# Three chunks of a projection in three fp32r matmuls, with the high part kept in the convolution's buffer

## What is computed

```python
conv = conv_b + sum(x_pad[:, k:k + L, :] * conv_w[k, 0] for k in range(K))   # K = L = 128
proj = conv @ Wp + bp                       # 512 -> 2 * 64
B_t, C_t = softplus(proj[..., :N]), tanh(proj[..., N:])
u = x @ Ws + bs
state = decay * state + dt * b_t * u_t;  y_t = c_t * state      # scan over time
x = x + y @ Wo + bo
h_next = tanh(h @ Wh + (x @ Wx + b)[t])                         # scan over time
out = x + h_next
```

## Time and profile before

| | |
|---|---|
| Runs | 1198.05 us median of 3 (1197.93 to 1198.36) |
| Profiled execution | 1197.2 us, of which the span of the trace is 1195.0 us |
| Granted PE clock, mean | 0.995 of full |
| Convolution of a chunk, 1st / others | 32.0 us / 29 to 30 us |
| Projection of a chunk, first transpose to the end of its last matmul | 41.6 us (chunk 2: 41.55) |
| First transpose of the four projections, at | 44.81, 116.53, 188.19, 259.74 us |
| Recurrence stage, from | 300.9 us |

### The profile page before, as it was taken

One profiled execution on the slowest core, in us unless ns is written; L12 is line 12 of the kernel. 1 busy time (PEld: TensorE's weight loads), 2 busy tenths in 40 slices (PEclk: granted clock), 3 DMA queues, 4 the chain that ended last, 5 costly groups with the idle time before them and its releaser, 6 DMA issues.

```text
span 1195.0 us, 16884 instructions
## 1 busy us (share of the span) xinstructions
PE 1164.7 (97%) x5888; PEld 938.6 (79%) x5888; DVE 682.7 (57%) x1104; ACT 532.8 (45%) x768; POOL 326.7 (27%) x175
## 2 busy tenths in 40 slices
PE   5999999999799999999999999999999999999997
PEld 5769587785588888888888888888888888888886
DVE  5565565556755555655555655555555555655553
ACT  2443535446235454544545354545445453545431
POOL 1000000014333333444333333334443333333340
PEclk9999999999899999999999999999999999999999
DMA  9909266261222222222322222222223222222202
GB/s 317 331 5 349 72 207 219 71 233 36 71 71 71 71 71 70 70 70 71 100 89 91 70 70 70 70 70 70 70 79 96 91 85 70 70 70 71 71 36 70
DMA packets 81462, 121.17 MB, mean 101 GB/s; under 512 B 3936, under 2 KB 39776, under 8 KB 81440
## 3 DMA queue, kind: packets, MB, share of 16 engines
q1 hardware_dynamic: 81440, 120.87, 31.1%
HBM read 87.30 MB, written 33.55 MB: 101 GB/s over the span
## 4 chain that ended last, share of the span: by engine, by line
PE 96%; DVE 1%; POOL 1%; DMA 1%; ACT 0%; issue 0%; SPq 0%; POOLq 0%; DVEq 0%
PE bank L639 10%; PE bank L708 10%; PE bank L716 10%; PE bank L717 10%; PE bank L720 10%; PE bank L702 10%; PE bank L701 9%; PE bank L660 9%; PE bank L652 5%; PE bank L744 5%; PE bank L691 2%; PE bank L683 2%; PE bank L692 2%; PE bank L677 2%; POOL x_lo L311 1%; DMA vec<-vectors 1%
## 5 line engine op out<-in xcount | busy, mean ns | idle before, releaser
L311 POOL TENSOR_TENSOR x_lo<-x_f,x_hi 128x512 fp32r<-128x512 f32 x126 | 159.5, 1297 | 561.9 <-ACT x_hi L403 561.9
L416 ACT ACTIVATE h_f<-z_f 128x512 f32<-128x512 f32 x128 | 80.9, 632 | 294.7 <-DVE z_f L588 294.7
L716 PE MATMUL bank<-wh_hi,hT_hi 128*128 128x512 f32 x512 | 200.4, 391 | 0.0
L702 PE MATMUL bank<-wx_lo,x_hi 128*128 128x512 f32 x512 | 200.2, 391 | 0.0
L717 PE MATMUL bank<-wh_lo,hT_hi 128*128 128x512 f32 x512 | 200.2, 391 | 0.0
L701 PE MATMUL bank<-wx_hi,x_hi 128*128 128x512 f32 x512 | 199.6, 390 | 0.0
L598 DVE TENSOR_TENSOR hT_lo<-bank,hT_hi 128x512 fp32r<-128x512 f32 x128 | 88.6, 692 | 187.0 <-ACT hT_hi L420 187.0
L588 DVE TENSOR_TENSOR z_f<-bank,b_rows 128x512 f32<-128x512 f32 x128 | 88.5, 692 | 130.3 <-PE bank L720 129.0
L305 POOL TENSOR_TENSOR x_lo<-x_f,x_hi 128x2048 fp32r<-128x2048 f32 x32 | 148.3, 4634 | 11.9 <-PE bank L652 11.9
L708 PE MATMUL bank<-wx_hi,x_lo 128*128 128x512 f32 x512 | 144.5, 404 | 1.5 <-DVE x_lo L581 1.1
L720 PE MATMUL bank<-wh_hi,hT_lo 128*128 128x512 f32 x512 | 137.0, 389 | 0.0
(11 more groups left out here) (71 smaller groups left out, 1472.2 us busy)
## 6 DMA issues: line engine op xcount, KB each, us to landing
x_ring<-x_rev SPq DMA_DIRECT2D x64, 512.0 KB, 8.0
x_f<-x_dtb SPq DMA_DIRECT2D x32, 1024.0 KB, 8.3
out<-x_f SPq DMA_DIRECT2D x31, 1024.0 KB, 5.4
t_ring<-hankel SPq DMA_DIRECT2D x64, 256.0 KB, 7.3
w_f<-Wx SPq DMA_DIRECT2D x1, 1024.0 KB, 5.5
w_f<-Wh SPq DMA_DIRECT2D x1, 1024.0 KB, 5.0
out<-x_f SPq DMA_DIRECT2D x4, 256.0 KB, 2.3
wp_now<-Wp SPq DMA_DIRECT2D x4, 128.5 KB, 2.0
```

The source lines that it names most:

```text
L311: nc.gpsimd.tensor_tensor(x1_lo[:, c], x1_f[:, par, c], f(x1_hi[:, c]), ALU.subtract)\
L702: nc.tensor.matmul(z, x1_hi[:, k, s], wx_lo[:, k], start=False, stop=False)
L716: nc.tensor.matmul(z, hT_hi[:, k], wh_hi[:, k], start=start and k == 0, stop=False)
```

## The change

Chunks 0 to 2 take a new path, `split_projection`; chunk 3 keeps the old one.

- POOL splits `Wp`'s rows into `wp_hi` and `wp_lo` and copies the bias to `conv_b` (`split_wp`), once for each of the three chunks.
- ACT writes `turned_hi` = TURN + bias, rounded to fp32r. It is kept for all 32 banks, in the addresses of `conv`: bank m goes where its four transposed blocks lay.
- DVE writes `turned_lo` = TURN + bias - `turned_hi`, with one instruction that reads the PSUM bank and `turned_hi`.
- PE multiplies three times in fp32r where it multiplied once in fp32: `wp_hi` by hi, `wp_lo` by hi, `wp_hi` by lo.
- PROJ's even banks are still added by DVE. Its odd banks are now copied by ACT: in chunk 0 straight into `bc` with the bias; in chunks 1 and 2 into `projected`, which is again the place of the same bank in `conv`, and from there POOL adds them to `bc`.
- As `conv` holds what POOL has still to add, ACT and DVE wait for POOL's 16 additions of chunk 1 (`odd_added`) before they copy banks of chunk 2's convolution into it, and likewise before chunk 3.
- `Ws` is loaded and split after `Wh` instead of at the start. DVE waits at the start for `wo_lo` (`weights_ready` 1), since `turned_lo` shares the place of `Wo`; ACT's wait for two such steps is gone. The loop over chunks is written out on ACT, DVE and POOL, and in part on PE and SP.

```diff
+            def split_wp(c):
+                pool.wait_ge(wp_loaded, DMA * (c + 1))
+                nc.gpsimd.tensor_copy(wp_hi[:], wp_f[:, 0:2 * P]).then_inc(wp_split, 1)
+                nc.gpsimd.tensor_copy(conv_b[:], wp_f[:, 2 * P:]).then_inc(wp_split, 1)
+                pool.wait_ge(wp_split, 3 * c + 1)
+                nc.gpsimd.tensor_tensor(wp_lo[:], wp_f[:, 0:2 * P], f(wp_hi[:]), ALU.subtract).then_inc(wp_split, 1)
+            split_wp(0)
+            for c in range(1, KC - 1):
+                split_wp(c)
+                for n in range(1, BANKS, 2):
+                    pool.wait_ge(odd_copied, BANKS // 2 * c + n // 2 + 1)
+                    cols = bass.ts(n, 512)
+                    nc.gpsimd.tensor_tensor(bc[:, cols], bc[:, cols], projected[:, n], ALU.add).then_inc(odd_added, 1)
...
+            def turned_to_hi(c):
+                act.wait_ge(wp_split, 3 * c + 3)
+                for m in range(BANKS + LAG + 1):
+                    if m > LAG and m % 2:
+                        copy_odd(c, m - LAG - 1)
+                    if m < BANKS:
+                        act.wait_ge(turn_done, BANKS * c + m + 1)
+                        nc.scalar.activation(turned_hi[:, m], TURN[m % 4][:], ACT.Identity, bias=conv_b[:])\
+                          .then_inc(hi_ready, 1)
+            def copy_odd(c, n):
+                act.wait_ge(proj_done, BANKS * c + n + 1)
...
+                    nc.scalar.copy(projected[:, n], PROJ[n % 4][:]).then_inc(odd_copied, 1)
...
-            act.wait_ge(weights_ready, 2)
+            turned_to_hi(1)
+            act.wait_ge(odd_added, BANKS // 2)
+            copy_conv(2)
+            turned_to_hi(2)
+            act.wait_ge(odd_added, BANKS)
...
+            def turned_to_lo(c, m):
+                dve.wait_ge(hi_ready, BANKS * c + m + 1)
+                if m >= 4:
+                    dve.wait_ge(proj_done, BANKS * c + m - 3)
+                nc.vector.scalar_tensor_tensor(out=turned_lo[:, m % 4], in0=TURN[m % 4][:], scalar=conv_b[:],
+                                               in1=f(turned_hi[:, m]), op0=ALU.add, op1=ALU.subtract)\
+                  .then_inc(lo_ready, 1)
...
+            fill_band(0, 0)
+            dve.wait_ge(weights_ready, 1)
+            chunk(0)
+            chunk(1)
+            dve.wait_ge(odd_added, BANKS // 2)
+            chunk(2)
+            dve.wait_ge(odd_added, BANKS)
...
+            def split_projection(c):
...
+                        pe.wait_ge(lo_ready, BANKS * c + n + 1)
+                        if n >= 4:
+                            pe.wait_ge(odd_copied if n % 2 else even_added, half * c + (n - 4) // 2 + 1)
...
+                        nc.tensor.matmul(PROJ[n % 4][:], hi, turned_hi[:, n], start=True, stop=False)
+                        nc.tensor.matmul(PROJ[n % 4][:], lo, turned_hi[:, n], start=False, stop=False)
+                        nc.tensor.matmul(PROJ[n % 4][:], hi, turned_lo[:, n % 4], start=False, stop=True)\
+                          .then_inc(proj_done, 1)
+                pe.wait_ge(even_added, half * (c + 1) - 1)
+                pe.wait_ge(odd_copied, half * (c + 1) - 1)
```

## The result

| | before | after |
|---|---|---|
| Runs, median (range), 4 each | 1197.99 us (1197.82 to 1198.36) | 1186.63 us (1185.99 to 1187.17) |
| Ratio to before, 95% interval | | 0.9903 (0.9891 to 0.9914) |
| Profiled execution / its span | 1197.2 / 1195.0 | 1186.3 / 1184.5 |
| Granted PE clock, mean | 0.995 | 0.996 |

The account below looks back on a forecast made before the run. PE, busy 97% of the span, was taken to bound the kernel. Three projections save 12.9 us, two boundaries cost 1.5: 11.4 off 1197.2 gives 1185.8, plus 0.85 for the median, 1186.7 us; range 1182.0 to 1191.5.

Parts of the forecast that it names:

- PE's period: Projections of chunks 0 to 2: transposes plus three fp32r matmuls take 1.155 us a bank, 0.14 less than before.
- the 0.47 for four transposes: Time of a bank's four transposes beside fp32r matmuls, taken from the recurrence, instead of 0.43 us beside fp32.
- first rival: Projections: transposes stay at 0.43 us as beside fp32, saving 3.4 us more, 1183.3 us; chance 20%.
- second rival: Projections: new semaphore waits and weight loads cost PE about 0.05 us more a bank, 4.8 in all, 1191.5 us; 12%.
- The first matmul: Start of each changed projection: first matmul waits for ACT then DVE, 2.20 us after the first transpose instead of 1.78.
- sum for a projection: One changed chunk's projection: start, 28 periods and four last banks take 37.26 us, 4.30 less than before.
- The others keep up: Inside projections DVE, ACT and POOL need less than PE's 2.31 us a pair of banks, so only PE shows.
- third rival: Projections of chunks 1 and 2: DVE slows beside POOL, costing some 11 us, 1198 us, no change; chance 4%.
- Boundaries: Into chunks 2 and 3, PE waits 0.77 us each for a band copy behind POOL's last addition; 1.5 us cost.
- The table load: Before chunk 3, ACT's 1.28 us load delays its first copy to 4.0; PE wants it at 4.4, so hidden.
- Start and end: DVE's wait for wo_lo at the start and Ws moved to the end cost nothing, bound 0.5 us.
- The total: Whole kernel: 12.9 us saved in projections less 1.5 at boundaries gives 11.4 us, median 1186.7 us.

Follow-up runs that it names:

- two passes: Changed kernel without the second of three matmuls (wp_lo by turned_hi), so that product is missing from the result: 1170.67 us, ratio 0.9777.
- DVE adds all: Changed kernel, but DVE adds the odd banks too, ACT and POOL do nothing with PROJ, and no odd_added waits: 1199.13 us, ratio 1.0007.
- two additions: Changed kernel, but POOL does each of its 32 additions twice, the first into a dead place: 1202.55 us, ratio 1.0037.
- reordered waits: Changed kernel with DVE's band copy and ACT's table load before the POOL wait, PE's Wp wait before its convolution-copy waits: 1183.76 us, ratio 0.9887.
- first experiment: Changed kernel, but DVE's first fill_band copy of chunks 2 and 3 is issued before the wait for POOL's additions: 1186.0 us, ratio 0.9897.
- the experiment with two SBUF inputs: Changed kernel plus an extra two-SBUF-input DVE addition per pair of banks, in two placements: 1185.86 us, and 1188.56 us one instruction later.

## Why the prediction was right

**PE's period: the mechanism right, the size 0.018 too long.** Predicted 1.155, measured 1.137, so PE does set the pace, but outside the 1.15 to 1.16 that the prediction had named as its sign. The term that was mis-sized is the 0.47 for four transposes. It came from a single row pair of the recurrence, 1.38 for four transposes and four matmuls; the neighbours there take 1.36 to 1.37, and in the changed kernel the four transposes and the matmul behind them take 0.35 + 0.31, which less one matmul's 0.23 leaves 0.43, the figure beside fp32. The three matmuls take 3 x 0.235. 28 periods in three chunks: 1.5 us more gain than I summed. The first rival's cheap transitions were thus what happened, half-way: the 0.43 holds, but a matmul's pitch is nearer 0.235 than 0.227. The second rival's small waits, 0.05 more a bank, don't show in this period.

**The first matmul: 2.35 for 2.20.** ACT starts 0.75 after the first transpose (0.67 in the earlier trace rows), and DVE 0.11 behind ACT's end, where 0.03 was summed from the earlier trace rows; the durations and the hop to PE are as summed. And the first matmuls of a projection are 0.34 apart where the others are 0.31. Together with the period this makes 37.19, 37.31 and 37.04 for a projection, where 37.26 was forecast. The period alone would have made it 0.5 shorter; 0.15 of the first matmul, 0.1 of the last four banks (3 x 0.235 each, not 0.68) and a later start of the next stage behind chunks 0 and 1 (0.12 and 0.26) went against that. So the sum for a projection is close by errors that cancel.

**The others keep up: right.** No PE wait for `turned_lo` but the first of each projection, POOL's additions 1.29, ACT and DVE idle in each period. The runs give the margins that the prediction only bounded: DVE 0.18 under PE's period with even banks alone (two passes), over it with all banks (DVE adds all), POOL 0.98 free in 2.27, and a loss at the boundary beyond that (two additions). The third rival fell with the one-input operations' unchanged 0.74 and 0.68 beside POOL.

**Boundaries: the mechanism right, 2.0 for 1.5.** The forecast was 0.77 twice. The PE waits measure 0.47 and 0.87. POOL's last addition is released and ends as summed (PE's last matmul to PE's release 2.65 and 2.70, for 2.58), but into chunk 2 PE itself starts 0.26 behind its last matmul, where its loop over chunks turns round, and its first record is 0.1 longer to the next; it waits that much less. The 0.26 stands in projection 1 instead (37.31 to the 37.04 of chunk 2). What I missed is 0.13 to 0.16 at each of three first transposes. PE's wait for `wp_split` (in chunk 3 for `wp_loaded`) stands behind the one for DVE's last copy, and can be passed only after it, though long fulfilled; where it stands first, 0.09 to 0.11 of this is gone. That the written order is the cause is not shown: in chunk 0 of the changed kernel the order is the same and costs nothing, and there the reordered waits cost 0.05.

**The table load: right.** It was summed as hidden, with 0.4 to spare behind a wait of 0.77. In the changed kernel ACT's first copy of chunk 3 ends at 220.96 and PE wants its fifth bank's place at 221.5, so it costs nothing, with 0.5 between. The spare time exists only behind the wait for `t_ring`: with that wait removed PE is 0.6 late (first experiment).

**Start and end: nothing, right.** The differences there (0.5 and 1.2 us, against each other) come and go in repeated traces of the changed kernel: its second trace has the first transpose at 44.89 for 44.30, and 893.9 for the recurrence.

**The total: nearer than the terms were.** 11.4 us were forecast and 11.4 measured. The projections gave 0.3 more than the 12.9 of the sum and the boundaries took 0.5 more than the 1.5; the start and the recurrence added 0.7 of scatter. Against that 0.9, the median lies 2.2 above the span of the profiled execution, where 3.05 had been taken (1197.2 - 1195.0 + 0.85). That these leave 0.1 us is luck; that the time lies in the range is not.

What stays open: why the first fp32r matmul behind transposes takes 0.31 to the next and the others 0.23 to 0.24, what makes PE's 0.26 at the loop's end here when the kernel before shows none, and what in the waits in front of the first transpose costs the 0.13 to 0.16.

## What to carry to other kernels

When one fp32 matmul is replaced by fp32r passes, the gain is PE's pitch and is easily read from any place that already runs such passes; whether it arrives is decided by the engine that must write the second half. Move its other work first: without the moved sums the whole 11 us were lost.

Whatever is handed to an engine off the path comes back at the next place that waits for its last item. Put there, ahead of that wait, all that doesn't depend on it (here a band copy and a table load, 1.8 us together with PE's own waits), and of several waits in a row try the one fulfilled last at the end: here it gave 0.09 to 0.11 us in three places and took 0.05 in a fourth.

## What the runs showed of the hardware

- fp32r matmuls of 512 columns stand 0.23 to 0.24 us apart, one fp32 matmul of the same shape takes 0.86, and three fp32r matmuls 0.70. The Trainium skill (FP8 and Floating Point Precision, TensorE Precision Notes) has true fp32 as four passes. A pass would be 0.215 by it and three of them 0.645, an estimate from that page and the 0.86; no row here shows a pass by itself, and the three matmuls measure 0.70.
- Busy time and pitch differ by engine and operation: on DVE 0.74 and 0.66 for a 128x512 operation with a pointer scalar (`turned_lo`, or PSUM plus bias), 0.68 and 0.60 for one with two tensors; on POOL 1.29 and 1.22 to 1.25 for 128x512 in fp32.
- Who starts first decides who is slowed between DVE and POOL. In the changed kernel DVE's band copy started 0.01 ahead of POOL's `wp_lo` in chunk 0, kept its 0.42, and POOL took 1.01. In chunk 2 POOL was first (151.80 to 152.53), and DVE's copy took 0.67. DVE's rows of the two, and POOL's of chunk 0:

```profile
84.33 0.42 DVE L523 COPY t_ring<-t_ring 64x512 f32<-64x512 f32 x1
...
152.14 0.67 DVE L523 COPY t_ring<-t_ring 64x512 f32<-64x512 f32 x1
```

```profile
84.34 1.01 POOL L306 TENSOR_TENSOR wp_lo<-turned,wp_hi 128x256 fp32r<-128x256 f32 x1
```

The copy of chunk 2 ends 0.28 after POOL's operation, as the operation held back in the experiment with two SBUF inputs did. In the first experiment, too, the band copy moved ahead of the wait (218.14) met POOL's last but one addition (217.38 to 218.67): it took 0.81 and ended 0.28 behind it.

- After PE had stood for 6.3 us (POOL's doubled additions), its granted clock was 0.50 from its restart at 157.54 to beyond 162. The waits of 0.47 and 0.87 in the changed kernel leave it at 1.00 (mean of the convolutions 2 and 3).
- Between the end of DVE's last copy and PE's first transpose lie 0.24 to 0.26 us in chunks 1 to 3 of the changed kernel, and 0.15 where the waits that are long fulfilled stand ahead of the late one. In the kernel before it is 0.10, with the late wait not the last one either, so the order alone does not set it.
